# Attention macaron block on one core: four of eight row transfers of a batch's queries begun by ScalarE

## What is computed

```
x = x + 0.5 * ffn(layernorm(x))     # ffn: real(ifft(fft(x) @ W)) + bias, the same as one 256x256 product
x = x + attn(layernorm(x))
x = x + 0.5 * ffn(layernorm(x))

attn: q, k, v = left @ Wq.T, left @ Wk.T, left @ Wv.T     # left: the first 128 of 256 columns
      energy = q k^T per head (16 heads of 8), softmax(energy / 4) over the keys
      out = softmax @ v, then @ Wo.T + bo
```

## Time and profile before

| | |
|---|---|
| median of 3 runs | 327.63 us (327.6 to 328.64) |
| the profiled execution | 325.67 us, of which the span of the trace is 323.8 us |
| TensorE busy | 300.8 us (93%) |
| ScalarE busy | 254.7 us (79%) |
| VectorE busy | 192.9 us (60%) |
| GpSimd busy | 97.7 us (30%) |
| granted TensorE clock | 0.999 of full |

### The profile page before, as it was taken

One profiled execution on the slowest core, in us unless ns is written; L12 is line 12 of the kernel. 1 busy time (PEld: TensorE's weight loads), 2 busy tenths in 40 slices (PEclk: granted clock), 3 DMA queues, 4 the chain that ended last, 5 costly groups with the idle time before them and its releaser, 6 DMA issues.

```text
span 323.8 us, 8951 instructions
## 1 busy us (share of the span) xinstructions
PE 300.8 (93%) x3461; PEld 114.9 (36%) x3465; DVE 192.9 (60%) x552; ACT 254.7 (79%) x280; POOL 97.7 (30%) x112
## 2 busy tenths in 40 slices
PE   8887899879999999999999999999999889898985
PEld 5643333223333433334333433343333223232333
DVE  1677655726785687666775778467845634361254
ACT  2100598989898989998998889898999998999921
POOL 6732441040532236043604052313500520043004
PEclk9999999999999999999999999999999999999999
DMA  7635949538566667549564946675364945012102
GB/s 202 240 132 183 197 122 208 180 101 166 151 239 191 162 134 262 187 163 173 195 198 150 177 150 241 172 179 115 132 198 167 159 133 166 33 67 65 35 32 67
DMA packets 30388, 50.40 MB, mean 156 GB/s; under 512 B 3840, under 2 KB 16512, under 8 KB 29440
## 3 DMA queue, kind: packets, MB, share of 16 engines
q1 hardware_dynamic: 28864, 48.13, 52.8%
q10 hardware_dynamic: 1472, 1.58, 2.2%
HBM read 31.87 MB, written 17.83 MB: 153 GB/s over the span
## 4 chain that ended last, share of the span: by engine, by line
PE 63%; DMA 11%; DVE 8%; SPq 7%; issue 5%; ACT 3%; ACTq 1%; POOL 0%; DVEq 0%
PE misc L694 23%; PE ot L785 22%; PE scores L772 12%; SPq L382 6%; DMA QS<-q_scr 6%; ACT probs L644 3%; DVE left_blocks L915 2%; PE scores L661 2%; DMA x_scr<-x_blocks 2%; DMA leftT<-left_scr 1%; DVE lh L906 1%; PE scores L694 1%; DMA xT<-x_scr 1%; PE scores L668 1%; DMA k_scr<-kp 1%
## 5 line engine op out<-in xcount | busy, mean ns | idle before, releaser
L644 ACT ACTIVATE probs<-scores 128x1024 f32<-128x1024 f32 x256 | 244.0, 1029 | 35.2 <-PE scores L772 35.0
L785 PE MATMUL ot<-probs,VS 128*32 128x512 f32 x1024 | 134.0, 595 | 5.3 <-ACT probs L644 4.1
L772 PE MATMUL scores<-QS,KS 32*128 32x512 f32 x512 | 64.9, 495 | 4.3 <-DMA QS<-q_scr 3.6
L772 PEld LDWEIGHTS scores<-QS,KS 32*128 32x128 f32 x512 | 24.7, 181 | 111.6 <-ACT probs L644 100.2
L785 PEld LDWEIGHTS ot<-probs,VS 128*32 128x32 f32 x1024 | 30.6, 109 | 29.7 <-ACT probs L644 9.4
L543 POOL TENSOR_TENSOR x_out<-x,half_bias 128x512 f32<-128x512 f32 x7 | 9.0, 1289 | 98.0 <-DVE x L961 98.0
L528 POOL TENSOR_SCALAR veps<-mv 128x4 f32<-128x4 f32 (+1 forms) x25 | 5.7, 229 | 95.2 <-DVE mv L895 95.2
L694 PE MATMUL misc<-half_ffn,xT 128*32 128x256 f32 x448 | 31.4, 385 | 1.5 <-DMA xT<-x_scr 1.5
L966 DVE SCALAR_TENSOR_TENSOR x_out<-misc,rstd,x_out 128x256 f32<-128x256 f32 x28 | 13.6, 484 | 31.7 <-PE misc L694 31.3
L694 PE MATMUL misc<-half_ffn,xT_in 128*32 128x256 f32 x400 | 27.9, 385 | 1.4 <-DVE half_ffn L1137 1.3
L530 POOL TENSOR_TENSOR rstd<-veps,power 128x4 f32<-128x4 f32 (+1 forms) x25 | 25.2, 1009 | 2.1
(11 more groups left out here) (109 smaller groups left out, 265.5 us busy)
## 6 DMA issues: line engine op xcount, KB each, us to landing
KS<-k_scr SPq DMA_DIRECT2D x56, 128.0 KB, 4.6
QS<-q_scr SPq DMA_DIRECT2D x56, 128.0 KB, 3.1
x_in<-x SPq DMA_DIRECT2D x8, 512.0 KB, 5.6
xT_in<-x_t SPq DMA_DIRECT2D x8, 512.0 KB, 7.1
k_scr<-kp SPq DMA_DIRECT2D x8, 512.0 KB, 2.6
q_scr<-qp SPq DMA_DIRECT2D x7, 512.0 KB, 3.7
x_scr<-x_blocks SPq DMA_DIRECT2D x7, 512.0 KB, 3.4
xT<-x_scr SPq DMA_DIRECT2D x7, 512.0 KB, 4.6
```

The lines of the kernel that those rows point to most:

```text
L644: nc.scalar.activation(probs[u % PRING][:, :, :], scores[u % SRING][:, :, :], ACT.Exp, scale=SCORE_SCALE).then_inc(exp_done, 1)
L772: last = mm(scores[(u + j // 2) % SRING][:, j % 2, :], KS[b % 2][rows, slot, kt * P:(kt + 1) * P].bitcast(F32R), QS[b % 2][rows, slot, :]. ...
L785: last = mm(ot[COL * j:COL * (j + 1), :], VS[b % 2][:, kt, h, :], probs[(u + j // 2) % PRING][:, j % 2, :], start=s % 8 == 0, stop=s % 8 == 7)
```

## The change

In batches it = 1 to 5 SP no longer begins the rows of lanes 2 and 3; ScalarE begins lane 2 ahead of the exponential s = 22 (slot 11), behind a wait for q_stored, and lane 3 ahead of s = 26 (slot 13), behind the same wait. Batches 0 and 6 keep their order, and nothing else is moved. As before, q_in waits on SP for q_stored in its second call too, now with no transfer behind it in these batches.

```diff
                 if it + 1 < B:
-                    q_in(it + 1, range(2, LANES))
+
+                    q_in(it + 1, range(2, LANES) if it in (0, B - 2) else ())
                 if it >= 1:
                     store_out(it - 1, 0)
...
                     if s == (2 * 10 if it else 2 * 6):
                         square(qp, sq_q, qp_step, it + 1)
+                if 1 <= it < B - 2 and s in (2 * 11, 2 * 13):
+                    act.wait_ge(q_stored, 16 * (it + 2))
+                    q_rows(act, (it + 1) % 2, slice(0, SLOTS), 2 if s == 2 * 11 else 3, rows_loaded)
                 act.wait_ge(scores_ready, u // 2 + 1)
```

## The result

The changed kernel takes 337.92 us in the median of 4 runs (337.04 to 338.54), the kernel before 328.13 us beside it (327.6 to 329.35, 4 runs). The ratio is 1.0316, with a 95% interval of 1.0274 to 1.0358: **3.2% slower**, where 334.4 us (2.1% above 327.63) had been forecast, with a range from 330.8 to 339.5.

The account below looks back on a forecast made before the run. The prediction took TensorE, busy for 93% of the span, to set the pace. Profiled 325.67 + 9.6 lost in slot 11 - 2.86 gained at batch ends = 332.4, plus 1.96 for the median: 334.4 us, range 330.8 to 339.5.

Parts of the forecast that it names:

- The sum: Whole kernel: profiled 325.67 plus 9.6 less 2.86 gives 332.4 us; with 1.96 for the runs' median, 334.4 us.
- 9.6 us lost in slot 11: Slot 11, batches 1 to 5: TensorE's value matmuls come 1.3 to 2.3 us late per batch, together 9.6 us.
- the landing of q's store: Ahead of s = 22: the store of q was taken to land in 2.8 to 3.8 us, 3.7 in batch 3.
- the pair of issues: Ahead of s = 22: two transfer issues on ScalarE's queue after q_stored, put at 1.36 us from the prologue.
- The room in slot 11: Slot 11, batch 3: ScalarE's exponentials were said to have 0.26 us before TensorE's value matmuls need them.
- landing minus 1.50: Slot 11: TensorE is late each batch by the landing time of q's store minus 1.50 us.
- Slot 13 costs nothing: Ahead of s = 26: the wait is long satisfied and the two issues run beside exponentials, cost taken as 0.
- The rival in which the engine stands still while the queue issues: Slot 13 too: ScalarE's engine stops during issues, adding 3.4 to 4.8 us, 337.8 to 339.2 us; chance 0.14.
- The 2.86 us at the end of a batch: End of batches 1 to 5: TensorE's waits for q rows and leftT all go, gaining 2.86 us in all.
- Two queues in each other's way: ScalarE's and SP's issues take turns, up to 1.2 us a batch, 340 us; chance 0.10, shared with rows still late.

Follow-up runs that it names:

- the issues without a wait: Against the change, ScalarE begins extra same-shape transfers from an input into a spare tile, without waiting for q_stored; SP begins all q rows: 339.47 us, ratio 1.0370.
- lane 3 alone: Against the kernel before, only lane 3 goes to ScalarE, ahead of s = 26; lane 2 stays with SP: 329.88 us, ratio 1.0052.
- both in slot 13: Against the changed kernel, lanes 2 and 3 are both begun by ScalarE ahead of s = 26, nothing ahead of s = 22: 333.86 us, ratio 1.0167.
- the kernel with lane 2 alone: Against the changed kernel, only lane 2 goes to ScalarE, ahead of s = 22; lane 3 stays with SP: 336.32 us, ratio 1.0255.

## Why the prediction was right, and where it wasn't

**Sign, place and most of the size were right.** The sum began with 9.6 us lost in slot 11; it is 10.06. By batch 1.6, 2.3, 2.2, 2.2 and 1.3 had been worked out, and 1.69, 2.03, 2.48, 2.79 and 1.07 were measured. The differences come from two inputs. One is the landing of q's store: 3.45, 3.79, 4.94, 4.29 and 2.83 us instead of 3.1, 3.8, 3.7, 3.7 and 2.8. The other is the pair of issues, for which the prediction took 1.36 us from the prologue (there with transfers of 32 KB, here of 128): it took 1.41 us in batches 3 and 4, in which SP's q rows begin at the same moment, and 1.14 or 1.15 in the others. In these rows the scores of slot 12 start 1.20 us after the pair has been issued, and before they started 4.10 us after the store of q was begun (165.17 - 161.07). So they are late by landing + pair - 2.90: 1.70, 2.03, 2.47 (with 0.98 less, because xT had held TensorE after the store had been begun), 2.80 and 1.07, the measured values to 0.01 us. That the sum of 9.6 came so near is in part luck: the landings were 2.2 us longer in all than assumed, and the shorter pairs (0.8 us) and xT (1.0) took most of that back. How long the store takes to land isn't set by the change alone: in traces of kernels in which ScalarE begins nothing it took 2.8 to 5.1 us. The room in slot 11 was read a little too small; s = 22 starts at 163.77 and s = 23 at 164.69 in the trace of before, so it is 0.34 us and not 0.26, which changes nothing in "landing minus 1.50", worked out from the whole distance.

**Slot 13 costs nothing** was right, and the ground given for it, that the queue hands on ahead of the engine, is shown by the issues without a wait: there the lead is a whole slot (92.94 against 95.15). The rival in which the engine stands still while the queue issues (337.8 to 339.2 us) met the time and not the mechanism.

**The step that failed is the sum's silence on the clock.** The prediction had TensorE idle for up to 2.3 us in a row and priced that at 2.3 us. Two of the five idle times brought 3.0 us more, at half the clock. Against the profiled execution the sum is short by 6.1 us (338.54 - 332.4): 3.0 for the clock, 2.1 for the other waits, 0.5 in slot 11, and 0.5 unnamed. As the median lies 3.5 us above the forecast and inside its range, the time alone wouldn't have shown that a term was missing.

**The 2.86 us at the end of a batch** came back in the changed kernel: nothing that is named in its batches is a wait for q rows or leftT. They did so for the reason given, that TensorE is late itself. In batch 3 leftT landed at 180.26 and was wanted at 181.89. Two things in that argument were wrong, and cost nothing here. leftT isn't begun when it was: it went out 7.48 us after q's store in batch 3, before 6.58, since SP's rows wait for the longer landing. And it landed 5.5, 5.5, 5.4, 4.4 and 4.6 us after its issue, for which the prediction had taken 4.65. That moving transfers to another queue gives up their place behind leftT was nowhere in it. The experiments without lateness in slot 11 (lane 3 alone, both in slot 13) show what the gain is then: negative. So 2.86 us are no gain of moving the issues; they come only where TensorE has lost more elsewhere.

**Two queues in each other's way** was priced as issues taking turns, up to 1.2 us a batch. That didn't happen (batch 3: two issues on ScalarE in 1.41 us from 172.37, four on SP in 2.41 from the same moment, as alone); what can be seen is 0.27 us more for ScalarE's pair where both begin at once. The Trainium skill's descriptor block that is locked for one use at a time (Perfetto Trace Analysis, DMA Instruction, HWDGE) can't account for more than that in these rows. Where the queues do meet is in the data: the Trainium skill says that transfers from all queues run on the same 16 DMA engines and interleave (DMA: Bandwidth & Descriptors, Issuing engines are not separate DMA queues), and leftT's landings agree with it. That would have been the rule to weigh.

Open are the 0.78 us in batch 1 of the changed kernel, which no releaser explains (one like it, 0.76 us, is at the same place in batch 1 of the kernel with lane 2 alone); what decides whether the clock falls behind an idle time, as its length alone doesn't; and the wait for xT in batch 3, which is also in traces of kernels that leave slot 11 alone.

## What to carry to other kernels

A transfer that is moved to a computing engine's queue brings its semaphore wait along, and everything behind it on that engine waits too: count from the landing of what it waits for, plus its issues, to the first instruction behind it that has no room. If the wait is satisfied when the queue gets there, the issues are free as long as the queue's lead lasts (two were free here, four cost 0.3 us). TensorE, made to wait, may lose more than the wait if its clock falls: look at the granted clock behind it. And before transfers leave a queue in which they stood behind a more urgent one, look at what that one's landing will be beside them.

## What the hardware showed that was not expected

- An idle time of TensorE in the middle of steady work brought the granted clock down to 0.50 behind it: after 1.97 and 2.74 us, not after 1.64, 2.42 and 1.01 in the same execution. In other traces it fell behind 1.76 us (issues without the wait) and stayed at 1.00 behind 1.92 (both lanes in slot 13). Filling the idle time with eight matmuls kept 1.00; the stretches at half the clock had cost 3.0 us.
- ScalarE's queue began transfers a slot before the exponential that they stand in front of in the program (92.94 against 95.15 for s = 22), so the slot written in the code isn't the time of the issue.
- Four transfers of 128 KB on a second queue, begun mostly in the 2.3 us ahead of it, changed the landing of a transfer of 256 KB on the first from 3.5 to 4.7 us to 5.2 to 6.3.
